# One K tile of layer 0 goes back from three bf16 products to one fp32 product, and four waits and a bank refill move, in a two-layer residual RNN

## What is computed

```python
xW = jnp.einsum('ntd,dh->nth', x, Wx) + b
def step(h_prev, xw_t):
    h_next = jnp.tanh(h_prev @ Wh + xw_t)
    return (h_next, h_next)
_, hs = jax.lax.scan(step, h0, jnp.swapaxes(xW, 0, 1))
# ...
x = x + layer0(x, cond_1024, Wx0, Wh0, b0)
x = x + layer1(x, cond_1024, Wx1, Wh1, b1)
```

## Time and profile before

| | |
|---|---|
| median of 3 runs | 2107.04 us (2106.73 to 2108.59) |
| the profiled execution's own time | 2108.59 us |
| its span, from first to last instruction | 2106.8 us |
| mean granted clock of TensorE | 0.997 |
| busy: TensorE matmul, weight load, VectorE, ScalarE | 98%, 86%, 82%, 53% |

### The profile page before, as it was taken

The page is one execution under the profiler, slowest core; times in us unless marked ns, Lnnn a source line. Parts: engine busy times, 40 slices in busy tenths (PEclk is TensorE's granted clock), DMA queues, the critical chain, the costliest instruction groups (busy, mean ns, idle before and its releaser), DMA issues.

```text
span 2106.8 us, 213809 instructions
## 1 busy us (share of the span) xinstructions
PE 2073.6 (98%) x98432; PEld 1802.2 (86%) x98432; DVE 1720.0 (82%) x10233; ACT 1121.5 (53%) x4609; POOL 14.2 (1%) x15
## 2 busy tenths in 40 slices
PE   7899999999999999999999999999999999999997
PEld 5788888888888888888888888888888888888886
DVE  3788888888888888888888888888888888888886
ACT  2455555555555555555555555555555555555553
POOL 2000000000000000000000000000000000000000
PEclk9999999999999999999999999999999999999999
DMA  3000000000000000000000000000000000000000
GB/s 102 25 23 27 25 25 26 24 27 23 27 23 27 25 24 27 23 27 23 27 24 25 25 24 27 23 27 23 27 24 25 26 24 27 23 27 23 27 25 15
DMA packets 112075, 56.20 MB, mean 27 GB/s; under 512 B 12448, under 2 KB 111024, under 8 KB 111536
## 3 DMA queue, kind: packets, MB, share of 16 engines
q1 hardware_dynamic: 111456, 53.53, 8.9%
q10 hardware_dynamic: 432, 1.18, 0.2%
q0 software_dynamic: 32, 0.02, 0.0%
HBM read 37.90 MB, written 16.78 MB: 26 GB/s over the span
## 4 chain that ended last, share of the span: by engine, by line
PE 98%; issue 1%; DVE 0%; DMA 0%; ACT 0%; SPq 0%; ACTq 0%; DVEq 0%
PE ps_rec L225 43%; PE ps_rec L238 33%; PE ps_xw L206 21%; DMA wx<-wx_in 0%; DVE zt L370 0%; DVE z L376 0%; ACT h L305 0%; SPq L177 0%; SPq L175 0%; ACT ps_rec L300 0%; DVE x_out L420 0%; DVEq L369 0%; ACTq L304 0%; ACTq L299 0%
## 5 line engine op out<-in xcount | busy, mean ns | idle before, releaser
L225 PE MATMUL ps_rec<-wh,h 128*32 128x128 f32 x32896 | 1265.1, 273 | 16.8 <-ACT h L305 12.3
L238 PE MATMUL ps_rec<-wh_part,h 128*32 128x128 bf16 x48960 | 1062.5, 221 | 9.0 <-issue 8.9
L305 ACT ACTIVATE h<-z 128x32 f32<-128x32 f32 x2048 | 470.5, 230 | 846.3 <-DVE z L376 829.5
L225 PEld LDWEIGHTS ps_rec<-wh,h 128*32 128x32 f32 x32896 | 830.3, 109 | 102.6 <-ACT h L305 17.9
L238 PEld LDWEIGHTS ps_rec<-wh_part,h 128*32 128x32 bf16 x48960 | 713.9, 96 | 193.0 <-issue 10.7
L384 DVE TENSOR_TENSOR h<-h 128x16 f32<-128x16 f32 x4080 | 627.2, 154 | 303.0 <-ACT h L305 302.6
L300 ACT ACTIVATE ps_rec<-ps_xw,mask 128x128 f32<-128x128 f32 x2048 | 670.7, 328 | 123.1 <-PE ps_xw L206 97.2
L370 DVE STREAM_TRANSPOSE zt<-ps_rec 128x128 f32<-128x128 f32 x2048 | 638.0, 311 | 39.5 <-PE ps_rec L238 22.3
L376 DVE TENSOR_REDUCE z<-zt 128x32 f32<-128x96 f32 x2048 | 545.9, 267 | 1.5 <-DVE zt L370 0.9
L206 PE MATMUL ps_xw<-wx,x_pe 128*32 128x128 f32 x8192 | 403.1, 273 | 3.3 <-DMA wx<-wx_in 2.4
L206 PE MATMUL ps_xw<-wx,x_mid 128*32 128x128 f32 x8192 | 401.9, 273 | 0.0
(11 more groups left out here) (14 smaller groups left out, 13.5 us busy)
## 6 DMA issues: line engine op xcount, KB each, us to landing
x_pe<-x_t SPq DMA_DIRECT2D x256, 64.0 KB, 1.9
x_dve<-x_t SPq DMA_DIRECT2D x256, 64.0 KB, 2.0
out_t<-x_out SPq DMA_DIRECT2D x256, 64.0 KB, 1.5
wx<-wx_in SPq DMA_DIRECT2D x4, 256.0 KB, 8.2
wh<-wh_in ACTq DMA_DIRECT2D x1, 1024.0 KB, 8.3
wh<-wh_in SPq DMA_DIRECT2D x1, 1024.0 KB, 4.8
wx<-wx_in SPq DMA_DIRECT2D x1, 1024.0 KB, 8.2
bias<-b_in ACTq DMA_DIRECT2D x2, 64.0 KB, 3.3
```

The costliest lines, as they stand in the source:

```text
L225: mm = pe.matmul(rows(bank, g), h_step(l, n - 1)[:, k, :], wh[l][:, k, g * P:(g + 1) * P], start=False, stop=k == KC - 1 and whole.start = ...
L238: mm = pe.matmul(rows(bank, g), h_bits(l, n - 1)[:, k, :], wh_part[l][:, i, at:at + P], start=False, stop=k == whole.start - 1 and i == PA ...
L305: act.activation(h_of(l, n), z[l][n % 2][:, :].rearrange("p (k b) -> p k b", k=KC), ACT.Tanh).then_inc(h_last if (l, n) == (0, T - 1) else ...
```

## The change

One more K tile of layer 0 is multiplied in fp32 (`KB` goes from (2, 2) to (1, 2)), so that VectorE splits 8 columns of layer 0's state in place of 16. ScalarE's waits for the loaded x and for the residual sums move from ahead of `begin(0)` to ahead of a tanh; VectorE's wait for `x_dve` moves from the slot with s modulo 4 equal to 0 to the first `sum_mid` of a chunk, one slot later; and `seed(1, c)` moves one slot earlier, from s modulo 4 equal to 3 to 2.

```diff
-KB = (2, 2)
+KB = (1, 2)
...
             def tanh(l, n):
+                c = n // S4 + 1 if l else (n + 6) // S4
+                if l == 0 and n % S4 == 2 and 2 <= c < NG:
+                    act.wait_ge(x_pe_loaded[c % 2], DMA * (c // 2))
+                if l == 1 and n % S4 == 0 and c < NG:
+                    act.wait_ge(mid_done, c + 1)
                 act.wait_ge(z_done[l], n + 1)
...
-                    if l == 0 and s % S4 == 1 and 2 <= (c := (s + 7) // S4) < NG:
-                        act.wait_ge(x_pe_loaded[c % 2], DMA * (c // 2))
-                    if l == 0 and s % S4 == 0 and 2 <= (c := s // S4) <= NG:
-                        act.wait_ge(mid_done, c)
                     if (n := number(l, s + 2)) is not None and n >= 2:
                         begin(l, n)
...
-                    if l == 1 and s % S4 == 3 and 2 <= (c := s // S4) < NG:
+                    if l == 1 and s % S4 == 2 and 2 <= (c := s // S4) < NG:
                         act.wait_ge(begun[1], S4 * (c - 1))
                         seed(1, c)
...
             def sum_mid(n):
                 c, t = n // S4, n % S4
+                if t == 0:
+                    dve.wait_ge(x_dve_loaded[c % 2], DMA * (c // 2 + 1))
...
             def sums(s):
-                c = (s + S4 - 1) // S4
-                if s % S4 == 0 and c < NG:
-                    dve.wait_ge(x_dve_loaded[c % 2], DMA * (c // 2 + 1))
```

## The result

The changed kernel takes 2162.8 us (median of 5 runs, 2160.74 to 2164.52) against 2107.04 us before: a ratio of 1.0263 with a 95% interval of 1.0249 to 1.0277. That is slower, by 55.4 us of 2107, and 7.2 us above the forecast of 2155.6, inside the range of 2144 to 2170. The profiled execution took 2160.57 us, its span is 2158.8 us and the mean granted clock 0.998, so the clock has no part in the difference.

The account below looks back on a forecast made before the run. TensorE was taken to set the pace, with the ring of a step hardly shorter. +47.8 (K tile) + 1.3 (seed) - 0.5 (program fetch) = +48.6 us on the profiled 2107.04 us median gave 2155.6 us, range 2144 to 2170.

Parts of the forecast that it names:

- The K tile: Layer 0's product on TensorE: one bf16 tile becomes fp32, +0.047 us a step over 1016 steps, +47.8 us.
- The split rival: Line 225's two tiles hide a 0.010 us wait for VectorE's split, which layer 0 loses: 2146 us, to 2140; 7%.
- The pace by instructions: TensorE's pace follows instruction count, so fewer records save 85 us, to 2022 us; 4% together with a milder form.
- The moved waits: ScalarE's waits for x and the sums, now ahead of a tanh where it is idle: price 0, bounds -1 to +1 us.
- The margin of the ring: Product, transpose, total, tanh, product: hardly shorter than TensorE's pace, which can take about 0.04 us of a late weight load.
- For layer 1, more margin: Layer 1's stretch between its products contains layer 0's product, so it grows by 0.047 us.
- The seed: On ScalarE, the moved seed makes the next tanh(0) 0.05 us late in 254 slots: +1.3 us, upper bound 27 us.
- the seed rival: The tanh behind the seed starts 0.10 late or more and delays TensorE: 2163 to 2181 us; 13%.
- Program fetch: TensorE's stops for issue in written-out turns and first loop passes shrink with fewer records: -0.5 us, bounds 0 to -2.

Follow-up runs that it names:

- e9: Kernel before with two more already met waits ahead of every begin(0), none ahead of a tanh; ratio 1.0001.
- e5: Kernel before with a second, long met wait ahead of every tanh of layer 0, written before the wait for VectorE's sum; ratio 1.0271.
- e6: Changed kernel with the wait for VectorE's sum written ahead of the moved wait at the tanh; ratio 1.0199.

## Why the prediction was right, and where its steps were not

The forecast of slower was right, and the time lies in the range, but partly because two errors had opposite signs.

- **The K tile: right in kind, 5 us too large.** The term was 0.047 us a step, 47.8 us. It measured 0.042, 42.3 us in 254 chunks. I had halved the two-tile group of line 238 (0.344 / 2 = 0.172), but the tile that goes saves 0.178, since the one that stays takes only 0.168; the exchange is 0.218 - 0.178, and 0.001 more at the turn of the loop. My bounds of 0.045 to 0.050 came from rounding alone and were too narrow.
- **The split rival: no.** Three fp32 tiles take 0.655 us, 0.218 each, so two take 0.437, and that is what the two of layer 1 take as a median. The 0.440 of the prediction was a mean, with the turn of the loop in it.
- **The pace by instructions: no.** Layer 0's half has fewer records and is longer. The Trainium skill, page "TensorE: Matmul & The Clock Gate", section "Back-to-back issue gap", with its 81 ns for a sustained pair of load and matmul, does not describe this stream: 12 bf16 matmuls in four columns take 0.168 us, 56 ns a quad.
- **The moved waits: the step that failed.** I wrote "Price 0, bounds -1 to +1 us", since the conditions are met and ScalarE is idle there. Both are true, and the two waits cost 14.5 us. It is not the condition but a second wait, written ahead of the one that comes last, that makes the tanh 0.07 us late. I had asked whether the signals come late and what is queued behind, and not what a second wait does between a signal and its instruction: there it is an instruction more, as the records show.
- **The margin of the ring: right.** That a tanh some hundredths late shows, and that TensorE takes the first of them by the lead of its loads, was read from the rows before, and it is why 0.07 us twice in four slots costs 14.5 us and not 254 x 0.14 = 36. "For layer 1, more margin" was right as well: without the tile the same waits cost 41.9 - 11.2 = 30.7 us.
- **The seed: right.** Forecast 0.05 us late and +1.3 us; found 0.06 late and 1.5 us or less. The tanh starts 0.20 behind the seed, an overlap of 0.07 with a seed of 0.27. The Trainium skill gives 93 ns in "ScalarE: Activation LUTs", section "What ACT_TABLE_LOAD costs"; here 0.074 is the median for a tanh behind a seed, and 0.093 that for a begin behind a tanh, in the kernel before. The sign that I had named for the seed rival, waits of line 225 for the tanh in the middle of the run, did appear (13 times, 3.8 us, against twice before), though the seed was not the cause: the sign could not tell one late tanh from another.
- **Program fetch: right in sign at the end of the run, its size not settled.** I gave -0.5 us, bounds 0 to -2. TensorE's own waits for issue fell from 14.0 us (17 times) to 9.7 us (15 times) in the changed kernel and 8.2 us (15 times) with the tile alone. But they are 9.2 us with the moves alone and 11.4 us in e9, whose TensorE programs are those of the kernel before, so most of that fall is not the tile's. A better measure is the stretch from the start of slot 1016 to layer 1's half of slot 1031, where the program is written out: 34.8 to 35.8 us in six runs without the tile, 32.8 to 34.0 in six with it in layer 0. That is about 2 us saved. Here are the changed kernel's rows, which answer to the earlier trace rows:

```profile
PE ps_rec L225 <- issue: 4.1, 6, 0.9
...
PE ps_xw L206 <- issue: 3.1, 3, 1.2
...
PE ps_rec L238 <- issue: 2.5, 6, 0.8
```

Sum: 42.3 for the tile, 0.058 x 254 = 14.8 for the order of the waits, 1.7 for seed and VectorE's wait, and -3.4 as what is left to the measured 55.4 us. Of this some 2 us are the stretch at the end; the rest is within the interval of the ratio, 3 us either way.

One thing stays open. Halves of more than 1.09 us turn up 2 times in 1500 us in the kernel before, with the tile alone, in both layers and with the extra wait behind; 13 times in the changed kernel, with the moves alone and in e5; 7 times in e6. They cost the changed kernel some 2.8 us of these 1500 and are part of its mean. They are no chance: they stand at the same slots in runs that share the code around them (338, 594 and 850 in the changed kernel and with the moves alone), 256 slots apart, in e5 mostly 64. In most of them one instruction, VectorE's sum or the tanh, starts 0.2 to 0.3 us later behind its signal than elsewhere. What holds it was not tried.

## What to carry to other kernels

Where a chain of small steps is as long as the busy engine's own round, price every wait on it, met or not: write the wait that comes last first, or put the other at an instruction that has slack (two met waits ahead of begin(0) cost nothing). Two edits that touch the same ring don't add up: one can pay for the other's margin, so time each alone and both together. And look at the chain and at the distance between a signal and its instruction by place in the loop; TensorE at 99% busy hid 14.5 us of such waits.

## What the runs showed of the hardware that was not expected

- Two waits at one ScalarE instruction: 0.03 us from the sum to the tanh when the sum's wait is written first, 0.09 to 0.10 us when it is second, with the same number of instructions. The second one is a semaphore instruction of its own in the records, and the tanh starts 0.062 to 0.067 us behind its start.
- TensorE's loop: with a body of 8 slots (16 halves of 48 matmuls, so 768 matmuls and 768 loads in the records) the turn costs about 0.04 us, with 736 of each (the tile alone) 0.05, with 704 of each (the tile in both layers) nothing. With 1536 of each TensorE stops 723 times in the run, in the loop mostly once in 128 matmuls and 128 loads, and the run takes 1.49 times as long. That it is the size of the body which decides fits these runs, but was not tried by itself.
